# Writing out the ring loops of a graph edge kernel on Trainium2: five hardware loops become straight-line code

## The chip, the cores and the metric

The kernel runs on one core of one Trainium2 chip. Its five engines are TensorE (PE in the profile; its weight loads are PEld), VectorE (DVE), ScalarE (ACT), GpSimd (POOL) and SyncE (SP). Each has its own instruction stream; they meet only in semaphores.
## The reference

There are 12,500 nodes of 64 features and 400,000 edges, sorted by destination.

```
h    = relu(layernorm(x))                       # 12500 x 64
feat = concat(h[dst], h[src] - h[dst])          # 400000 x 128
m    = relu(feat @ W1 + b1) @ W2 + b2           # 400000 x 64
agg  = segment_max(m, dst);  agg = 0 where a node has no edge
out  = x + agg
```

The kernel splits feat @ W1 into a part A of the destination node and a part B of the source node, so that an edge needs relu(A[dst] + B[src]) @ W2. A and B are tables of 12,500 rows in DRAM.

## The kernel before

**Before the ring.** A and B are computed and stored; `a_edges` (400,000 rows) is filled with zeros, and A's row of each node is scattered to that node's first edge. B is also held in SBUF as three bf16 parts (`table`).

**The ring.** Each of the 128 partitions has 3125 edges in order. They are worked on in 260 chunks of 12 edges per partition (1536 edges), and a tail of 5. `RING` = 26 slots of `rows` hold chunks in flight, and `ITERS` = 10 rounds of 26 chunks are the 260 chunks. For chunk c:

- SP: `load_a` waits until `a_fill` is free and loads the chunk of `a_edges` (L333, L334); then it waits for the slot's gathers and loads the indices of the chunk one round later (L342, L343).
- POOL: 11 indirect DMAs gather B[src] for 11 of the chunk's 12 edges (`gather_chunk`, L393). It works up to one round ahead: before it refills a slot, POOL waits for `z_turned` of the chunk that had it, that is until TensorE has transposed it (L436), and for the new indices (L437).
- The 12th edge's B row is picked on TensorE: VectorE splits the index (`split_src`, L920 and L921), ScalarE spreads the keys (L537, L540), TensorE turns them (`turn_keys`, L666), VectorE compares them (`match_keys`, L935), TensorE picks with 37 matmuls of 128x512 into `ps_g` (`pick`, L676), ScalarE masks (`mask`, L549) and VectorE reduces (`choose`, L944).
- DVE: `fill` carries A's row along the edges of a node (12 instructions, L885), `add` forms A + B (L897), `maximum` runs the segmented maximum (12 instructions, L911).
- PE: 6 transposes (L687, they raise `z_turned`), 21 picks, 6 x 2 products with W2 (L696), the key turn (L666) and 16 more picks, the last of which raises `picked`.
- ACT: flags (L530, L531), keys, relu of the transposed sums (L560, waits for `z_turned`), 8 masks (L549), and the store of the chunk's maxima (L567).

In one step, picks are for a chunk 3 ahead and keys for one 5 ahead, so the engines form a loop over neighbouring steps: VectorE's match waits for `picked` of two chunks before; ScalarE's relu for `z_turned`; TensorE's products for the relu.

**What sets the order.** The program is written by hand, engine by engine. Each engine has a hardware loop over the rounds (`Fori`), whose body holds 26 chunks. The round `i` is a register. A semaphore's target that depends on `i`, as `(i * RING + k - RING + 1) * GROUPS`, and an address in DRAM that depends on it, are worked out in registers as the program runs.

Of the kernel before, what the change touches and what calls it, by code (L numbers as in the profile page):

```python
# [18 lines left out]
def edge_conv(nc, x, src, dst, W1, b1, W2, b2, out):  # L19
    N, C = x.shape  # L20
    E = src.shape[0]
    TILES = E // P
    CHUNK = 12
    RING = 26
    ITERS = TILES // (CHUNK * RING)
# [3 lines left out]
    W = CHUNK * C  # L29
# [14 lines left out]
    AE_RING = 2  # L44
# [20 lines left out]
    with ExitStack() as ctx:  # L65
# [18 lines left out]
        state = sb("state", [P, 2, W])  # L84
        zt = sb("zt", [P, GROUPS, 512])
        src_idx = sb("src_idx", [P, RING, CHUNK], I32)
        same = sb("same", [P, TILES + (FILL_AHEAD + 1) * CHUNK])
# [127 lines left out]
        a_loaded = [sem(f"a_loaded{s}") for s in range(AE_RING)]  # L215
# [40 lines left out]
        src_lanes = src.rearrange("(p t) -> p t", p=P)  # L256
        dst_lanes = dst.rearrange("(p t) -> p t", p=P)
        dst_blocks = dst.rearrange("(b k) -> b k", k=BLOCK)
        a_lanes = a_edges.rearrange("(p t) c -> p (t c)", p=P)
# [16 lines left out]
        def _(sp):  # L276
# [55 lines left out]
            def load_a(c, k, tiles=CHUNK):  # L332
                sp.wait_ge(a_free, c + 1)  # L333
                sp.dma_start(a_fill[:, k % AE_RING, 0:tiles * C],  # L334
                             a_lanes[:, bass.ds(c * W, tiles * C)]).then_inc(a_loaded[k % AE_RING], 16)

            with sp.Fori(0, ITERS - 1) as i:
                for k in range(RING):
                    load_a(i * RING + k, k)

                    sp.wait_ge(gathered[k], (i + 1) * 16 * GATHERED)  # L342
                    sp.dma_start(src_idx[:, k, :], src_lanes[:, bass.ds((i * RING + RING + k) * CHUNK, CHUNK)]  # L343
                                 ).then_inc(src_loaded[k // 2], 16)
            for k in range(RING):
                load_a((ITERS - 1) * RING + k, k)
# [22 lines left out]
        def _(pool):  # L369
# [59 lines left out]
                in_=a_table, in_offset=at(dst_all[:, :], 1)).then_inc(ends_gathered, 16)  # L429
            scatter_a(BATCH, NJ)  # L430
            gather_chunk(RING - 1)
            with pool.Fori(1, ITERS) as i:
                for k in range(RING):

                    pool.wait_ge(z_turned, (i * RING + k - RING + 1) * GROUPS)
                    pool.wait_ge(src_loaded[k // 2], (i + 1) * 32)  # L436

                    pool.sem_inc(chunk_open, 1)
                    gather_chunk(k)
# [22 lines left out]
        def _(act):  # L462
# [63 lines left out]

            def flags(c, k, tiles=CHUNK):

                now = same[:, bass.ds(c * CHUNK, CHUNK)]
                nc.scalar.activation(keep[:, k % KEEP, 0, :], now, ACT.Relu)  # L530
                nc.scalar.activation(keep[:, k % KEEP, 1, :], now, ACT.Copy, scale=FLT_MAX).then_inc(keep_ready, 1)  # L531

# [20 lines left out]
            def step(c, k, tiles=CHUNK):  # L553
                if tiles == CHUNK:
                    flags(c + FILL_AHEAD, k + FILL_AHEAD)
                    spread_keys(c + KEYS_AHEAD, k + KEYS_AHEAD)
                for g, n in groups(tiles):
                    act.wait_ge(z_turned, c * GROUPS + g + 1)
                    full = n // 2 * P
                    last = nc.scalar.activation(zt[:, g, 0:full], ps_t[:, g, 0:full], ACT.Relu)  # L560
                    if n % 2:
                        last = nc.scalar.activation(zt[0:C, g, full:full + P], ps_t[0:C, g, full:full + P], ACT.Relu)
                    last.then_inc(relu_done, 1)
                if tiles == CHUNK:
                    mask(c + CHOOSE_AHEAD, k + CHOOSE_AHEAD)
                act.wait_ge(max_step, c * CHUNK + tiles + 1)
                act.dma_start(state_lanes[:, bass.ds(c * W, tiles * C)], state[:, k % 2, 0:tiles * C]  # L567
                              ).then_inc(state_stored[k % 2], 16)

# [26 lines left out]
            for c in range(CHOOSE_AHEAD):  # L597
# [1 line left out]
            act.wait_ge(a_scattered, 16 * NJ)  # L599
            nc.scalar.activation(a_rows[0:NP, :, :], b2_rows[0:NP, :].rearrange("p (o c) -> p o c", o=1)  # L600
                                 .to_broadcast((NP, NJ, C)), ACT.Copy, scale=-1.0).then_inc(maxima_preset, 1)
            with act.Fori(0, ITERS) as i:
                for k in range(RING):
                    step(i * RING + k, k)
            step(CHUNKS, 0, TAIL)
# [5 lines left out]
        def _(pe):  # L611
# [95 lines left out]
            for c in range(-KEYS_AHEAD, 0):  # L707
                turn_keys(c + KEYS_AHEAD, c + KEYS_AHEAD)
                if c >= -PICK_AHEAD:
                    pick(c + PICK_AHEAD, c + PICK_AHEAD, range(PAGES))  # L710
            with pe.Fori(0, ITERS) as i:
                for k in range(RING):
                    step(i * RING + k, k)
            step(CHUNKS, 0, TAIL)
# [8 lines left out]
        def _(dve):  # L723
# [244 lines left out]
            add(0, 0, 0, 0)  # L968
            choose(1, 1)
            fill_all(1)  # L970
            with dve.Fori(0, ITERS) as i:
                for k in range(RING):
                    c = i * RING + k
                    if k + 1 < RING:
                        add(c + 1, k + 1, i, i)
                    else:
                        add(c + 1, 0, i + 1, (i + 1) % ITERS)
                    prepare_picks(c, k, i)
                    fill_ready(c + 2, (k + 2) % RING, i + (k + 2) // RING)

                    dve.wait_ge(state_stored[k % 2], (i * (RING // 2) + k // 2 + 1) * 16)
                    for t in range(CHUNK + LEAD):
                        if t == CHUNK - 2:
                            choose(c + CHOOSE_AHEAD, (k + CHOOSE_AHEAD) % RING)
                        if t < CHUNK:
                            fill(c + 2, (k + 2) % RING, t)
                        if t >= LEAD:
                            maximum(c, k, t - LEAD)
# [45 lines left out]
```

## Time and profile before

| | |
|---|---|
| median of 3 runs | 5047.05 us (5042.66 to 5049.33) |
| the profiled execution | 5046.15 us, of which the span of the trace is 5044.3 us |
| PE, PEld busy | 3240.3 us (64%), 1876.2 us (37%) |
| POOL busy | 3109.6 us (62%) |
| DVE busy | 2493.6 us (49%) |
| ACT busy | 1025.4 us (20%) |
| mean granted TensorE clock | 0.794 of full speed |
| the chain that ended last | "another core or an unknown queue" 41%, "issue" 28%, DVE 10%, ACT 9%, PE 7% |

The first 737 us are the preparation; the ring then runs to about 4890 us, and the end of the kernel (last maxima, output) takes the rest. No engine is busy for more than 64% of the span, and the largest part of the chain is a releaser that the profile can't name. So the shares don't say what limits the ring; the rows of a few chunks must.

### The profile page before, as it was taken

Reading aid. Unit: us, or ns where it says so; the run is one execution under the profiler, and the core shown is the slowest. Engines: PE = TensorE matmul, PEld = TensorE weight load, DVE = VectorE, ACT = ScalarE, POOL = GpSimd, SP = SyncE. Lnnn points to the kernel's source line nnn. Section 1 sums busy time; section 2 is a strip of 40 time slices with the busy share of each in tenths; the row PEclk is TensorE's granted clock in tenths of the full one; section 3 lists DMA queues with packets and bytes.
Section 4 is the critical chain, followed back from the end, with each engine's and each line's share of the span. In section 5 each row is a group of like instructions: output and inputs, shape, how many; then the busy total and the mean of one; then the engine's idle time right before and its main releaser. Section 6 shows DMA issues by size and latency. Waiting matters only on the chain.

```text
span 5044.3 us, 58734 instructions
## 1 busy us (share of the span) xinstructions
PE 3240.3 (64%) x14598; PEld 1876.2 (37%) x14861; DVE 2493.6 (49%) x8363; ACT 1025.4 (20%) x4057; POOL 3109.6 (62%) x3186
## 2 busy tenths in 40 slices
PE   2100137777777777777777777777777777777970
PEld 2100014444444444444444444444444444444540
DVE  4100115555555555555555555555555555556871
ACT  4300212212122121221212222122221212212320
POOL 5777756666666666666666666666666666664017
PEclk8555558888888888888888888888888888888985
DMA  7866312222222222222222222222222222222222
GB/s 274 315 229 227 115 32 73 67 73 70 70 73 67 73 70 70 70 70 73 70 70 69 70 73 69 70 70 69 73 67 73 70 70 72 69 72 71 80 77 56
DMA packets 239614, 452.86 MB, mean 90 GB/s; under 512 B 94781, under 2 KB 95402, under 8 KB 238738
## 3 DMA queue, kind: packets, MB, share of 16 engines
q1 hardware_dynamic: 97663, 225.75, 14.2%
q0 software_dynamic: 103216, 117.29, 11.1%
q10 hardware_dynamic: 38362, 105.62, 5.4%
q8 instruction: 140, 2.29, 0.2%
q14 instruction: 233, 1.91, 0.1%
HBM read 230.84 MB, written 217.71 MB: 89 GB/s over the span
## 4 chain that ended last, share of the span: by engine, by line
another core or an unknown queue 41%; issue 28%; DVE 10%; ACT 9%; PE 7%; POOL 2%; ACTq 2%; DMA 1%; DVEq 1%; POOLq 0%; SPq 0%
ACT dst_all L549 5%; DVE state L911 4%; PE ps_g L676 4%; DVE a_fill L885 3%; PE ps_m L696 2%; POOL a_rows L456 2%; ACT zt L560 2%; ACTq L567 1%; DMA shared<-in_x_dram 1%; DVE rows L897 1%; ACT zt L474 1%; ACT keep L531 1%; PE ps_t L687 0%; ACT shared L501 0%
## 5 line engine op out<-in xcount | busy, mean ns | idle before, releaser
L393 POOL DMA_INDIRECT rows<-b_table,src_idx x2865 | 2785.5, 972 | 1523.6 <-issue 805.7
L676 PE MATMUL ps_g<-shared,dst_all 128*128 128x512 bf16 x9468 | 2318.6, 400 | 174.3 <-issue 170.5
L676 PEld LDWEIGHTS ps_g<-shared,dst_all 128*128 128x128 bf16 x9731 | 1011.1, 105 | 1329.5 <-issue 417.3
L696 PE MATMUL ps_m<-w_diag,zt 128*128 128x128 f32 x3126 | 707.8, 411 | 920.2 <-ACT zt L560 917.8
L696 PEld LDWEIGHTS ps_m<-w_diag,zt 128*128 128x128 f32 x3126 | 638.2, 308 | 1056.3 <-ACT zt L560 1049.8
L911 DVE SCALAR_TENSOR_TENSOR state<-state,keep,ps_m 128x64 f32<-128x64 f32 x3125 | 862.3, 276 | 202.5 <-PE ps_m L696 166.7
L885 DVE SCALAR_TENSOR_TENSOR a_fill<-a_fill,keep 128x64 f32<-128x64 f32 x3144 | 879.6, 280 | 53.1 <-DVE a_fill L885 41.6
L935 DVE TENSOR_TENSOR dst_all<-ps_s,page_keys 128x1664 bf16<-128x1664 f32 x132 | 249.6, 1891 | 816.0 <-remote 795.1
L935 DVE TENSOR_TENSOR dst_all<-ps_x,page_keys 128x1664 bf16<-128x1664 f32 x132 | 249.6, 1891 | 794.7 <-remote 774.7
L560 ACT ACTIVATE zt<-ps_t 128x512 f32<-128x512 f32 (+1 forms) x521 | 226.4, 486 | 1517.9 <-remote 1511.6
L549 ACT ACTIVATE dst_all<-ps_g,dst_all 128x64 f32<-128x64 f32 x2096 | 458.1, 347 | 33.2 <-DVE rows L944 33.2
L530 ACT ACTIVATE keep<-same 128x12 f32 (+1 forms) x263 | 55.9, 213 | 1662.2 <-issue 929.0
L666 PE MATMUL ps_s<-dst_all,ones_h 128*128 128x128 f16 x133 | 40.2, 302 | 442.4 <-ACT dst_all L540 440.9
L897 DVE TENSOR_TENSOR rows<-rows,a_fill 128x512 f32<-128x512 f32 (+1 forms) x522 | 269.1, 557 | 33.2 <-issue 33.2
L944 DVE TENSOR_REDUCE rows<-dst_all 128x64 f32<-128x512 f32 x262 | 267.9, 1023 | 0.0
L687 PE MATMUL ps_t<-ident,rows 128*128 128x128 f32 x1563 | 213.5, 273 | 1.4 <-issue 1.4
L853 DVE TENSOR_TENSOR a_fill<-a_fill,shared 128x512 f32<-128x512 f32 x26 | 18.0, 693 | 383.3 <-issue 372.3
L687 PEld LDWEIGHTS ps_t<-ident,rows 128*128 128x128 f32 x1563 | 186.8, 141 | 53.0 <-issue 3.5
L666 PEld LDWEIGHTS ps_s<-dst_all,ones_h 128*128 128x128 f16 x133 | 19.2, 145 | 442.8 <-issue 440.0
L447 POOL DMA_INDIRECT head<-states,lane_i x1 | 0.9, 942 | 261.2 <-DMA states<-state 261.2
L401 POOL DMA_INDIRECT rows<-in_dst_dram,blk_idx x101 | 102.6, 1016 | 73.5 <-issue 24.4
L419 POOL DMA_INDIRECT a_edges<-a_rows,first_idx x100 | 108.8, 1088 | 31.3 <-issue 31.3
(116 smaller groups left out, 877.0 us busy)
## 6 DMA issues: line engine op xcount, KB each, us to landing
a_edges<-state SPq DMA_DIRECT2D x80, 1250.0 KB
a_fill<-a_edges SPq DMA_DIRECT2D x260, 384.0 KB
states<-state ACTq DMA_DIRECT2D x260, 384.0 KB
rows<-b_table,src_idx POOLq DMA_INDIRECT x2865
src_idx<-in_src_dram SPq DMA_DIRECT2D x234, 6.0 KB
shared<-in_x_dram SPq DMA_DIRECT2D x5, 625.0 KB
b_table<-shared ACTq DMA_DIRECT2D x5, 625.0 KB
a_table<-a_rows SPq DMA_DIRECT2D x1, 3125.0 KB
```

The source lines that it names most:

```text
L393: nc.gpsimd.indirect_dma_start(out=rows[:, slot, t * C:(t + 1) * C], out_offset=None, in_=b_table, in_offset=at(src_idx[:, slot, :], t)).t ...
L419: nc.gpsimd.indirect_dma_start(out=a_edges, out_offset=at(first_idx, j), in_=a_rows[:, j, :], in_offset=None, bounds_check=E - 1, oob_is_e ...
L549: last = nc.scalar.activation(masked[:, o, :], ps_g[:, k % 2, o * C:(o + 1) * C], ACT.Copy, scale=octet_is[:, k % RING, o:o + 1])
L560: last = nc.scalar.activation(zt[:, g, 0:full], ps_t[:, g, 0:full], ACT.Relu)
L676: last = nc.tensor.matmul(ps_g[:, half, :], key_is[:, half, g, :], table[:, g, t, :], start=(g, t) == (0, 0), stop=g == PAGES - 1)
L687: last = nc.tensor.transpose(ps_t[0:m * C, g, a * C:a * C + P], rows[:, k, t * C:(t + m) * C], ident[:, :])
L696: last = nc.tensor.matmul(ps_m[:, g, a * C:(a + m) * C], zt[0:m * C, g, a * C:a * C + P], w2_pair[0:m * C, 0:m * C], start=True, stop=True)
L885: nc.vector.scalar_tensor_tensor(here, before, keep[:, k % KEEP, 0, t:t + 1], here, ALU.mult, ALU.add).then_inc(fill_step, 1)
L897: nc.vector.tensor_tensor(rows[:, k, part], rows[:, k, part], a_fill[:, k % AE_RING, part], ALU.add).then_inc(z_ready, 1)
L911: nc.vector.scalar_tensor_tensor(state[:, half, t * C:(t + 1) * C], before, keep[:, k % KEEP, 1, t:t + 1], ps_m[:, g, r * C:(r + 1) * C], ...
L935: nc.vector.tensor_tensor(key_is[:, half, :, :], ps_k[half].rearrange("p (o e) -> p o e", o=1).to_broadcast((P, PAGES, P)), page_keys[:, : ...
L944: nc.vector.tensor_reduce(rows[:, k, W - C:W], masked[:, :, :].rearrange("p o c -> p c o"), AX_X, ALU.add).then_inc(chosen, 1)
```

## The change

Every `Fori` over the rounds becomes a Python `for`, so `i` is a number when the program is built. The 26-chunk body is written out ten times on ACT, PE and DVE, and nine times on POOL and SP, with each semaphore target and address a constant. What is computed, the waits' targets and the order of engine instructions and DMAs stay as they are. The loop over the clearing of `a_edges` at L315 stays a hardware loop.

```diff
-                             a_lanes[:, bass.ds(c * W, tiles * C)]).then_inc(a_loaded[k % AE_RING], 16)
-
-            with sp.Fori(0, ITERS - 1) as i:
+                             a_lanes[:, c * W:c * W + tiles * C]).then_inc(a_loaded[k % AE_RING], 16)
+
+            for i in range(ITERS - 1):
                 for k in range(RING):
                     load_a(i * RING + k, k)
...
-                    sp.dma_start(src_idx[:, k, :], src_lanes[:, bass.ds((i * RING + RING + k) * CHUNK, CHUNK)]
+                    sp.dma_start(src_idx[:, k, :], src_lanes[:, (i * RING + RING + k) * CHUNK:(i * RING + RING + k + 1) * CHUNK]
...
-            with pool.Fori(1, ITERS) as i:
+            for i in range(1, ITERS):
...
-                now = same[:, bass.ds(c * CHUNK, CHUNK)]
+                now = same[:, c * CHUNK:(c + 1) * CHUNK]
...
-            with act.Fori(0, ITERS) as i:
+            for i in range(ITERS):
...
-            with pe.Fori(0, ITERS) as i:
+            for i in range(ITERS):
...
-            with dve.Fori(0, ITERS) as i:
+            for i in range(ITERS):
```

The instructions of VectorE at the start of the ring: the loop's entry, then chunk 0 up to its match. ISA and REGISTER_ALU are register work, [waits ...] names the semaphores that the row waits for. Before:

```order
L971 ISA
L891 ISA [waits fill_step]
L894 REGISTER_ALU [waits gathered1]
L897 TENSOR_TENSOR rows<-rows,a_fill 128x512 [waits chosen]
L897 TENSOR_TENSOR rows<-rows,a_fill 128x256
L918 REGISTER_ALU
L919 REGISTER_ALU [waits src_loaded2]
L920 TENSOR_SCALAR key_bits<-src_idx 128x1 [waits keys_spread]
L921 TENSOR_SCALAR key_bits<-src_idx 128x1
L933 REGISTER_ALU
L934 REGISTER_ALU [waits keys_turned]
L935 TENSOR_TENSOR dst_all<-ps_s,page_keys 128x1664 [waits picked]
```

And the same place now:

```order
L897 TENSOR_TENSOR rows<-rows,a_fill 128x512 [waits chosen,gathered1,fill_step]
L897 TENSOR_TENSOR rows<-rows,a_fill 128x256
L920 TENSOR_SCALAR key_bits<-src_idx 128x1 [waits keys_spread,src_loaded2]
L921 TENSOR_SCALAR key_bits<-src_idx 128x1
L935 TENSOR_TENSOR dst_all<-ps_s,page_keys 128x1664 [waits picked,keys_turned]
```

The register rows are gone, and the semaphores they waited for stand at the next engine instruction; the order of the others is the same. In one round VectorE's loop body held 415 REGISTER_ALU and 47 ISA, some 18 a chunk.

GpSimd at its loop's entry, the first slots refilled. Before:

```order
L393 DMA rows<-b_table,src_idx 128x64 x11
L432 UNCONDITIONAL_BRANCH
L432 ISA
L436 ISA [waits z_turned]
L393 DMA rows<-b_table,src_idx 128x64 [waits src_loaded0]
L393 DMA rows<-b_table,src_idx 128x64 x10
L435 ISA
```

And now:

```order
L393 DMA rows<-b_table,src_idx 128x64 x11
L393 DMA rows<-b_table,src_idx 128x64 [waits z_turned,src_loaded0]
L393 DMA rows<-b_table,src_idx 128x64 x10
L393 DMA rows<-b_table,src_idx 128x64 [waits z_turned,src_loaded0]
L393 DMA rows<-b_table,src_idx 128x64 x10
```

One register instruction a chunk is gone on GpSimd; its 11 gathers and the two semaphores it waits for are the same.

## Rows read from the trace of the kernel before

**Rows 1.** Windows: span; busy us (count) by engine; PEclk, DMA share, GB/s.

```profile
2035.00:2467.00 432.00, 318.22 (x1430) 185.22 (x1456) 237.47 (x807) 89.38 (x365) 276.25 (x286) 0.84 0.27 70
4760.00:4780.00 20.00, 19.90 (x112) 11.51 (x113) 18.08 (x63) 6.56 (x29) 0.00 (x0) 1.00 0.25 80
```

**Rows 2.** Timeline, two chunks: start us, us, engine, line, operation, [idle before <-releaser].

```profile
2500.12 0.87 ACT L560 ACTIVATE zt<-ps_t 128x512 f32<-128x512 f32 x2 [6.58 <-remote]
...
2500.93 0.94 POOL L393 DMA_INDIRECT rows<-b_table,src_idx  x1 [2.77 <-remote]
...
2502.18 0.98 POOL L393 DMA_INDIRECT rows<-b_table,src_idx  x1 [0.31 <-issue]
...
2508.68 0.82 PE L687 MATMUL ps_t<-ident,rows 128*128 128x128 f32 x6
...
2513.83 0.94 POOL L393 DMA_INDIRECT rows<-b_table,src_idx  x1 [0.30 <-issue]
2516.72 0.87 ACT L560 ACTIVATE zt<-ps_t 128x512 f32<-128x512 f32 x2 [6.63 <-remote]
2516.74 1.89 DVE L935 TENSOR_TENSOR dst_all<-ps_x,page_keys 128x1664 bf16<-128x1664 f32 x1 [7.32 <-remote]
...
2517.54 0.94 POOL L393 DMA_INDIRECT rows<-b_table,src_idx  x1 [2.77 <-remote]
...
2534.16 0.94 POOL L393 DMA_INDIRECT rows<-b_table,src_idx  x1 [2.78 <-remote]
```

**Rows 3.** Timeline, last round of the ring, after GpSimd's last gather.

```profile
4748.35 1.88 DVE L935 TENSOR_TENSOR dst_all<-ps_s,page_keys 128x1664 bf16<-128x1664 f32 x1
...
4755.81 0.82 PE L687 MATMUL ps_t<-ident,rows 128*128 128x128 f32 x6
...
4758.38 1.88 DVE L935 TENSOR_TENSOR dst_all<-ps_x,page_keys 128x1664 bf16<-128x1664 f32 x1
...
4759.04 0.85 ACT L560 ACTIVATE zt<-ps_t 128x512 f32<-128x512 f32 x2
```

**Rows 4.** Waits from 700 to 4800 us: waiter <- releaser: us, times, longest.

```profile
ACT zt L560 <- remote: 1511.6, 233, 7.4
DVE dst_all L935 <- remote: 1490.1, 228, 32.4
...
POOL rows L393 <- remote: 677.9, 234, 3.3
```

**Rows 5.** Sequencer instructions by line: count: duration ns min/median/max.

```profile
L881 DVEq ALU_OP  x2860: 13/40/697, 744.1 to 4885.7; - x191
...
L905 DVEq FUSED_REGOPS  x260: 46/46/64, 745.7 to 4881.8; - x130
...
L334 SPq FUSED_REGOPS  x234: 42/43/703, 697.8 to 4562.9; - x117
...
L435 POOLq FUSED_REGOPS  x216: 37/37/37, 743.0 to 4582.6; - x108
...
L711 PEldq COMPARE_BRANCH  x10: 83/4306/4822, 1157.1 to 4882.8; - x10
```

**Rows 6.** Timeline across a turn of the loops (near 2453 to 2459 us).

```profile
2450.87 0.94 POOL L393 DMA_INDIRECT rows<-b_table,src_idx  x1 [3.17 <-remote]
...
2461.28 1.03 DVE L897 TENSOR_TENSOR rows<-rows,a_fill 128x512 f32<-128x512 f32 x2 [2.96 <-issue]
...
2466.61 1.89 DVE L935 TENSOR_TENSOR dst_all<-ps_s,page_keys 128x1664 bf16<-128x1664 f32 x1 [4.18 <-remote]
2466.67 0.87 ACT L560 ACTIVATE zt<-ps_t 128x512 f32<-128x512 f32 x2 [1.52 <-remote]
...
2467.56 0.94 POOL L393 DMA_INDIRECT rows<-b_table,src_idx  x1 [3.18 <-remote]
...
2484.30 0.94 POOL L393 DMA_INDIRECT rows<-b_table,src_idx  x1 [3.01 <-remote]
```

More of the change, by code:

```diff
@@ L566, in step @@
                 act.wait_ge(max_step, c * CHUNK + tiles + 1)
-                act.dma_start(state_lanes[:, bass.ds(c * W, tiles * C)], state[:, k % 2, 0:tiles * C]
+                act.dma_start(state_lanes[:, c * W:c * W + tiles * C], state[:, k % 2, 0:tiles * C]
                               ).then_inc(state_stored[k % 2], 16)
```

## Prediction

> **What bounds the kernel now.** I read the slices of the page first, then windows, two chunks of the timeline, the waits, and last the sequencers' own instructions.
>
> The windows show two regimes. While GpSimd gathers, a round of 26 chunks takes 432 us, 16.6 us a chunk, and no engine is full: PE is busy for 318 of the 432 us, POOL for 276, DVE for 237. After the last gather PE is busy for 19.90 of 20 us at full clock [rows 1], and a chunk takes 4758.38 - 4748.35 = 10.03 us [rows 3]. That stage is bound by TensorE's own work. Some 234 chunks are of the first kind and 26 of the second.
>
> In the first regime the timeline shows a fixed beat. The relus start at 2500.12 and 2516.72, 16.60 us apart; GpSimd's first gathers of a chunk at 2500.93, 2517.54 and 2534.16, 16.61 and 16.62 us apart [rows 2]. Each beat is made of GpSimd's parts: 11 gathers at 1.25 us from start to start (the first at 2500.93, the eleventh at 2513.83, ending at 2514.77), then 2.77 us of waiting. 2514.77 - 2500.93 = 13.84, and with 2.77 it is 16.61.
>
> What is it that GpSimd waits for? By the code `z_turned`, raised by TensorE's transposes. Those run from 2508.68 to 2509.50, yet ScalarE's relu, which waits for the same semaphore, starts at 2516.72, 7.2 us after they end, and VectorE's match, which waits for `picked`, at 2516.74 [rows 2]. GpSimd follows 0.8 us later. In the stage without gathers the relu starts 4759.04 - 4756.63 = 2.4 us after the transposes [rows 3]. So three engines on three semaphore waits come free together, about 2 us after GpSimd's last gather of the chunk ends, and only while it gathers. The profile has no name for what holds TensorE's signals back ("remote"), in 233 of ScalarE's waits (1511.6 us), 228 of VectorE's and 234 of GpSimd's [rows 4]. I take it as a beat that GpSimd's 11 gathers set: burst, release, next burst. Whatever the other engines do within 16.6 us ends in a wait.
>
> **The change part by part.** The sum is made against the profiled execution, 5046.15 us (span 5044.3); the median of the runs shown is 5047.05, 0.9 us above it.
>
> *Register work on VectorE.* 415 + 47 instructions a round are 18 a chunk, at 40 ns (L881) to 46 ns (L905) [rows 5]: 18 x 40 = 0.72 us a chunk of sequencer time, 187 us over 260 chunks. They run while the datapath is busy with the instruction before, or within the wait of 7.32 us before the match [rows 2]. Value: 0. If that cover were gone it would be all of 0.72 us in the 234 chunks, 168 us. In the last stage PE is full, so it is 0 there too.
>
> *Register work on the others.* SyncE loses some 5 to 6 a chunk at about 43 ns (L334) and GpSimd 1 at 37 ns (L435) [rows 5]; the one on GpSimd is issued ahead, while gathers are running. TensorE loses 3 and ScalarE 6 a chunk (83 and 159 a round in the order of instructions), which I price like the row of L435. All lie ahead of a wait. Value: 0; together at most 15 x 0.04 = 0.6 us a chunk, 140 us, if all of it stood in the beat, which no row suggests.
>
> *The wait itself.* GpSimd needs 0.81 us from the release seen on ScalarE (2516.72) to its first gather (2517.54). It waits for the same two semaphores after the change, before the same DMA, so that stays, as do the 11 gathers: they had constant addresses already. Bounds: 0 below, and above the 37 ns of its register instruction, 9 us over 234 chunks.
>
> *The turns.* A branch on TensorE takes 4.31 us in the median, ten times [rows 5]. At the turn shown VectorE comes to its add 2.96 us late, and then waits 4.18 us for the match instead of 7.32, ScalarE 1.52 us for the relu instead of 6.63: the waits absorb it [rows 6]. GpSimd's beats across that turn are 2467.56 - 2450.87 = 16.69 and 2484.30 - 2467.56 = 16.74 us against 16.61: 0.08 + 0.13 = 0.21 us a turn, 1.9 us for nine. If the waits didn't cover them, 4.31 x 9 = 39 us would come back. I take 1.9, since the beats across the turn show it directly.
>
> The Trainium skill has a rule that speaks for more ("Runtime: NRT & Kernel Launch", Instruction fetch mechanics): fetch runs ahead in straight order, a taken branch out of the loaded pages stalls for a fetch, and therefore kernels prefer to be unrolled. The 4.31 us of the branch agrees with the stall. By that rule alone the sum would be 39 us; by the rows of the beat it is 2.
>
> *Entry of the loops.* Around 697 to 707 us some of SyncE's register instructions take up to 0.70 us each (the maximum of L334) [rows 5]. Five or six of them before the first chunk would be 3 to 4 us if TensorE waited behind them; 0 if not. I take 1.
>
> *Code.* The straight-line code is longer as a program, but every instruction of a loop was executed ten times anyhow; the number executed falls by the register work. No added wait, no added DMA, no order changed. Value 0.
>
> Sum: 1.9 + 1 = 2.9 us off: 5043.3 for a profiled execution, 5044 us for a median.
>
> **The rivals.**
>
> *A. The turns are exposed.* Then 39 us come off, 5008 us. For it: branches of 4.31 us. Against it: the shrunken waits of rows 6. Chance 0.10.
>
> *B. The beat gets shorter.* If TensorE's signals are held back because something that all the sequencers share is loaded (they all fetch and signal), removing the register work relieves it. For it: up to 0.70 us for a register instruction that has a median of 43 ns, on an engine that touches no data [rows 5]; the hold has no other name. Against it: the beat follows GpSimd's gathers, which don't change. A beat shorter by the 0.04 to 0.72 us of the bounds above gives 9 to 168 us, 4879 to 5038; were the hold gone altogether, GpSimd would be at 13.84 + 0.3 of issue gap, 2.47 us shorter in 234 chunks: 578 us, 4468. Chance 0.20 in all, of which 0.03 is the whole hold, and about half stands in the first 55 us.
>
> *C. The beat gets longer: slower.* The gathers' hold is met sooner: VectorE and TensorE, rid of 0.72 us a chunk, raise `picked` and `z_turned` earlier in the burst, and if each held signal costs a further step of the 0.70 us that the longest register instructions took [rows 5], the beat is 17.3 us in 234 chunks: +164 us, 5211. One chunk in three of that is 55 us, 5102. It decides once GpSimd's first gathers stand more than 16.62 us apart. Against it: the beat was the same whether VectorE's match came free with the relu or not. Chance 0.12 for slower by over 0.2%.
>
> *D. The change doesn't do what it says.* The order of instructions shows that it does; 0.
>
> **How the numbers follow.** My forecast, the beat unmoved, has 0.58. Two runs of this kernel differ by up to 7 us, so under 0.2% (10 us) can't be told from no change. The forecast's own range is 5034 to 5054, nearly all of it within 0.2%. A (0.10) and B (0.20) are faster; the forecast lends a little to each side. Faster 0.31, same 0.55, slower 0.14. The range goes down to A and into B's first third, 4990, and up to 5062, a part of C: 0.58 + 0.10 + 0.10 + 0.03, about 0.8.
>
> **What would show it.** Right: GpSimd's first gathers still 16.6 us apart, ScalarE's relu still some 7 us behind the transposes' end, the last stage still at 10.03 us a chunk, DVE's and ACT's waits longer by what the register work was, and no beat of 16.7 at the old turns. A would show as rounds shorter by 4 us at the turns alone. B or C would show as another beat in every chunk, with GpSimd's wait of 2.77 us shorter or longer and its gathers still 1.25 us apart. The forecast is wrong if that wait changes by more than 0.05 us a chunk.

## The result, and the profile after

The changed kernel is slower: 5086.52 us in the median of six runs (5072.64 to 5103.61), against 5044.82 us (5039.43 to 5049.33) for the kernel before on the same chip, ratio 1.0089 with a 95% interval of [1.0066, 1.0112]. The forecast was 5044 with a range of 4990 to 5062, and slower had a chance of 0.14. The profiled execution took 5083.08 us, its span is 5081.3 us, 37.0 us above the span before; the granted clock is nearly the same (0.796 against 0.794). The change did what it says: 50,057 instructions instead of 58,734, and no register instruction left on PE, ACT or DVE.

The page's groups of the kernel after. Columns: busy us, mean ns of one | idle us before it, and what ended most of that.

```profile
L676 PE MATMUL ps_g<-shared,dst_all 128*128 128x512 bf16 x9468 | 2498.8, 410 | 643.0 <-issue 620.0
L911 DVE SCALAR_TENSOR_TENSOR state<-state,keep,ps_m 128x64 f32<-128x64 f32 x3125 | 860.0, 275 | 1370.6 <-remote 1023.0
L560 ACT ACTIVATE zt<-ps_t 128x512 f32<-128x512 f32 (+1 forms) x521 | 232.7, 483 | 748.3 <-remote 697.4
L393 POOL DMA_INDIRECT rows<-b_table,src_idx x2865 | 2777.2, 969 | 1565.5 <-issue 835.0
```

The same groups on the page of before, which were not shown ahead:

```profile
L676 PE MATMUL ps_g<-shared,dst_all 128*128 128x512 bf16 x9468 | 2318.6, 400 | 174.3 <-issue 170.5
L911 DVE SCALAR_TENSOR_TENSOR state<-state,keep,ps_m 128x64 f32<-128x64 f32 x3125 | 862.3, 276 | 202.5 <-PE ps_m L696 166.7
L560 ACT ACTIVATE zt<-ps_t 128x512 f32<-128x512 f32 (+1 forms) x521 | 226.4, 486 | 1517.9 <-remote 1511.6
L393 POOL DMA_INDIRECT rows<-b_table,src_idx x2865 | 2785.5, 972 | 1523.6 <-issue 805.7
```

Read the last row of each first. GpSimd's gathers take as long as before (8 us less in all), and its idle time ahead of them grew by 41.9 us: 33.6 of the 37.0 us stand there. By the gathers' starts and ends, the ring's first one starts 2.7 us later, from there to the end of the ring's last one it takes 3914.4 us instead of 3886.4, and what follows is 6.2 us longer. Then see how the waits of the others changed places. VectorE used to wait ahead of the key match [rows 4] and hardly ahead of its maxima (202.5 us); now it waits 1370.6 us ahead of the maxima, and TensorE, which waits for nothing the profile can name ("issue"), has 643.0 us of gaps between picks instead of 174.3. These two rows don't say where the time went: the kernel before, run again (e5 below), has 864.2 us ahead of the maxima too, and e8, which is faster than before, has 521.3 us of TensorE's gaps.

GpSimd's waits from 700 to 4800 us, kernel after, answering to [rows 4]. Columns: waiter <- releaser: us in total, times, longest.

```profile
POOL rows L393 <- issue: 746.9, 2379, 8.1
POOL rows L393 <- remote: 457.0, 167, 4.8
POOL rows L393 <- PE ps_t L687: 273.5, 36, 38.1
```

Before, 234 waits of 2.90 us in the mean ended "remote", one at each chunk's end. Now only 167 do, and 36 end at TensorE's transposes; without the first one (38.1 us, ahead of the ring; 35.2 us before) those are 35 waits of 6.7 us. Between them are places where GpSimd does not wait at all: from the starts of its gathers, 35 times 22 gathers follow each other without a pause, which never happened in the profile before.

The price of such a pair can be added up from the 233 pauses between bursts. Before they are 2.90 us in the mean, 675 us together. After, 36 are under 1 us (0.32 us in the mean), the pause that follows one of these is 6.7 us in the mean, and the others are 2.9 us as before: 714 us together. So a pair first saves 2.6 us and then costs 3.8 us, 1.3 us net, and 36 of them explain the 39 us by which the pauses grew.

One such pair, the third of the 35, in the timeline after (start us, us, engine, line, operation, [idle before <-releaser]):

```profile
904.89 1.89 DVE L935 TENSOR_TENSOR dst_all<-ps_s,page_keys 128x1664 bf16<-128x1664 f32 x1 [1.94 <-remote]
...
909.83 1.11 ACT L560 ACTIVATE zt<-ps_t 128x512 f32<-128x512 f32 x2 [6.20 <-remote]
...
911.34 0.94 POOL L393 DMA_INDIRECT rows<-b_table,src_idx  x1 [2.99 <-remote]
...
915.43 0.82 PE L687 MATMUL ps_t<-ident,rows 128*128 128x128 f32 x6
...
917.99 1.88 DVE L935 TENSOR_TENSOR dst_all<-ps_x,page_keys 128x1664 bf16<-128x1664 f32 x1
...
919.26 0.60 ACT L560 ACTIVATE zt<-ps_t 128x512 f32<-128x512 f32 x1 [0.51 <-remote]
...
925.33 0.94 POOL L393 DMA_INDIRECT rows<-b_table,src_idx  x1 [0.30 <-issue]
...
929.91 0.58 PE L676 MATMUL ps_g<-shared,dst_all 128*128 128x512 bf16 x1 [3.29 <-issue]
...
931.31 0.61 PE L676 MATMUL ps_g<-shared,dst_all 128*128 128x512 bf16 x1 [0.82 <-issue]
...
932.74 0.59 PE L676 MATMUL ps_g<-shared,dst_all 128*128 128x512 bf16 x1 [0.82 <-issue]
...
937.82 0.94 POOL L393 DMA_INDIRECT rows<-b_table,src_idx  x1 [0.30 <-issue]
...
942.70 0.28 DVE L911 SCALAR_TENSOR_TENSOR state<-state,keep,ps_m 128x64 f32<-128x64 f32 x1 [21.75 <-remote]
...
946.98 1.06 POOL L393 DMA_INDIRECT rows<-b_table,src_idx  x1 [8.21 <-PE ps_t L687]
```

At 904.89 VectorE gets its picks in the middle of GpSimd's burst, so it meets the match about 5 us ahead of ScalarE's relu; in [rows 2] both came free together after the burst. (Alone this breaks nothing, as e5 shows below.) Its part is then already done when the relu comes (909.83), and the next chunk runs fast: the relu is again at 919.26, 9.4 us later, as in the stage that TensorE bounds. So `z_turned` is there before GpSimd's burst, begun at 911.34, has ended. GpSimd goes on without a pause (0.30 us before the gather at 925.33), to 938.76. In the second half of these 22 gathers TensorE crawls: single matmuls 1.40 and 1.43 us apart, with 0.82 us of gap though they wait for no semaphore. Its next transposes, which come after these picks, start only at 944.68, and so GpSimd itself waits 8.21 us for them. VectorE gets the products of TensorE only at 942.70, after 21.75 us, though the last of the twelve started at 924.92: that signal was late, whatever TensorE's pace. The windows around it (span, then busy us (count) of PE, PEld, DVE, ACT, POOL; granted clock, DMA share, GB/s), the first to be held against [rows 1]:

```profile
2035.00:2467.00 432.00, 318.69 (x1427) 167.32 (x1452) 237.27 (x814) 89.21 (x364) 271.35 (x282) 0.84 0.26 70
4790.00:4810.00 20.00, 19.89 (x112) 11.46 (x113) 18.00 (x62) 6.64 (x28) 0.00 (x0) 1.00 0.24 78
894.00:920.00 26.00, 21.20 (x108) 12.45 (x111) 17.36 (x60) 7.57 (x29) 17.32 (x18) 0.93 0.25 68
920.00:947.00 27.00, 13.30 (x43) 5.57 (x43) 5.07 (x23) 2.02 (x9) 14.22 (x17) 0.62 0.16 35
918.00:924.00 6.00, 4.43 (x24) 2.72 (x23) 2.77 (x7) 3.23 (x12) 4.55 (x5) 1.00 0.57 158
930.00:936.00 6.00, 2.87 (x5) 0.45 (x5) 0.00 (x0) 0.00 (x0) 4.48 (x6) 0.50 0.15 30
```

The 27 us of the crawl hold 43 matmuls against 108 in the 26 us ahead, and the granted clock is 0.62 against 0.93. The clock did not start the crawl: it is still at its full level (1.00, 2.4 GHz) from 918 to 924, where the first single matmul stands after a gap (922.81), and at the lower one (0.50, 1.2 GHz) from 930, after TensorE had worked for only 0.62 of 6 us. A late fetch of code doesn't set the pace either: the pages count 271 packets in the two instruction queues after and 373 before, and the one such packet that the trace has in the crawl, at 932.98, lies between matmuls that are 1.40 us apart ahead of it (929.91 and 931.31) and behind it (938.37 and 939.77).

The long window of 432 us shows nothing: a round that lost and one that didn't look alike in it, POOL's 282 gathers against 286 aside. The last stage is unchanged at 4816.34 - 4806.31 = 10.03 us a chunk, its relu 4806.97 - 4804.56 = 2.4 us behind the transposes, as in [rows 3]:

```profile
4803.74 0.82 PE L687 MATMUL ps_t<-ident,rows 128*128 128x128 f32 x6
4806.31 1.88 DVE L935 TENSOR_TENSOR dst_all<-ps_s,page_keys 128x1664 bf16<-128x1664 f32 x1
4806.97 0.85 ACT L560 ACTIVATE zt<-ps_t 128x512 f32<-128x512 f32 x2
...
4816.34 1.88 DVE L935 TENSOR_TENSOR dst_all<-ps_x,page_keys 128x1664 bf16<-128x1664 f32 x1
```

### The profile page after: what moved, and what is told of

It is laid out like the page before. It is cut to its first block, busy times and chain, and to the rows that moved or that the text cites. A ratio compares the mean times of both kernels' runs of the same rounds, so it can differ in the third digit from the quotient of the medians.

```text
span 5081.3 us, 50057 instructions
## 1 busy us (share of the span) xinstructions
PE 3251.7 (64%) x14598; PEld 1711.5 (34%) x14861; DVE 2484.5 (49%) x8363; ACT 1026.7 (20%) x4057; POOL 3098.0 (61%) x3186
## 3 DMA queue, kind: packets, MB, share of 16 engines
q14 instruction: 153, 1.25, 0.1%
## 4 chain that ended last, share of the span: by engine, by line
another core or an unknown queue 30%; PE 27%; issue 21%; DVE 13%; ACT 5%; POOL 2%; DMA 1%; ACTq 0%; DVEq 0%; POOLq 0%; SPq 0%
PE ps_g L676 20%; PE ps_m L696 6%; DVE state L911 5%; DVE a_fill L885 5%; POOL a_rows L456 2%; PE ps_t L687 2%; ACT dst_all L549 1%; DVE rows L897 1%; ACT zt L560 1%; DMA shared<-in_x_dram 1%; ACT zt L474 1%; ACT dst_all L540 1%; ACT shared L501 0%; ACTq L567 0%
## 5 line engine op out<-in xcount | busy, mean ns | idle before, releaser
L676 PE MATMUL ps_g<-shared,dst_all 128*128 128x512 bf16 x9468 | 2498.8, 410 | 643.0 <-issue 620.0
L676 PEld LDWEIGHTS ps_g<-shared,dst_all 128*128 128x128 bf16 x9731 | 987.7, 103 | 1979.3 <-issue 1132.4
L911 DVE SCALAR_TENSOR_TENSOR state<-state,keep,ps_m 128x64 f32<-128x64 f32 x3125 | 860.0, 275 | 1370.6 <-remote 1023.0
L696 PE MATMUL ps_m<-w_diag,zt 128*128 128x128 f32 x3126 | 525.5, 326 | 388.3 <-ACT zt L560 251.4
L696 PEld LDWEIGHTS ps_m<-w_diag,zt 128*128 128x128 f32 x3126 | 479.9, 233 | 493.4 <-ACT zt L560 308.5
L530 ACT ACTIVATE keep<-same 128x12 f32<-128x12 f32 x263 | 55.9, 212 | 2406.3 <-DVE state L911 1737.6
L687 PE MATMUL ps_t<-ident,rows 128*128 128x128 f32 x1563 | 245.9, 290 | 55.7 <-issue 54.9
L687 PEld LDWEIGHTS ps_t<-ident,rows 128*128 128x128 f32 x1563 | 203.4, 150 | 136.2 <-issue 93.0
```

The costliest lines, as they stand in the source:

```text
L676: last = nc.tensor.matmul(ps_g[:, half, :], key_is[:, half, g, :], table[:, g, t, :], start=(g, t) == (0, 0), stop=g == PAGES - 1)
L687: last = nc.tensor.transpose(ps_t[0:m * C, g, a * C:a * C + P], rows[:, k, t * C:(t + m) * C], ident[:, :])
L696: last = nc.tensor.matmul(ps_m[:, g, a * C:(a + m) * C], zt[0:m * C, g, a * C:a * C + P], w2_pair[0:m * C, 0:m * C], start=True, stop=True)
L911: nc.vector.scalar_tensor_tensor(state[:, half, t * C:(t + 1) * C], before, keep[:, k % KEEP, 1, t:t + 1], ps_m[:, g, r * C:(r + 1) * C], ...
```

## The experiments

Ratios are to the kernel before on the same chip, where it took 5011 us for e1 to e8 and 5053 to 5057 us for e9 to e18. The last columns are counted in the profiled execution, over the 234 chunks of the ring in which GpSimd gathers: the mean time from GpSimd's first gather of a chunk to that of the next (its beat), the times from one key match to the next that are over 22 us, the pairs of bursts that GpSimd issued without a pause (one or two more or less by what is called a pause, in e12 from 18 to 30), and the relus of ScalarE that start before the burst under way has ended.

| run | what | ratio, 95% | beat | over 22 us | pairs | relus in a burst |
|---|---|---|---|---|---|---|
| before | | | 16.62 | 0 | 0 | 2 |
| after | all five written out | 1.0089 [1.0066, 1.0112] | 16.74 | 51 | 35 | 116 |
| e1 | SyncE alone | 1.0009 [0.9998, 1.0019] | 16.50 | 5 | 4 | 14 |
| e2 | TensorE alone | 1.0042 [1.0022, 1.0062] | 16.58 | 14 | 12 | 47 |
| e3 | VectorE alone | 1.0102 [1.0071, 1.0134] | 16.61 | 45 | 33 | 117 |
| e4 | ScalarE alone | 1.0006 [0.9997, 1.0016] | 16.48 | 3 | 2 | 10 |
| e5 | before again | 1.0004 [0.9995, 1.0014] | 16.49 | 3 | 3 | 12 |
| e6 | after, 11 registers a chunk in VectorE's fill waits | 1.0047 [1.0033, 1.0061] | 16.54 | 47 | 31 | 116 |
| e7 | before, 8 gathers a chunk | 0.8049 [0.8037, 0.8062] | 12.29 | 0 | 0 | 12 |
| e8 | after, GpSimd waits for its own gathers | 0.9790 [0.9776, 0.9803] | 16.03 | 11 | 0 | 107 |
| e9 | before, with that wait | 1.0000 [0.9990, 1.0009] | 16.68 | 0 | 0 | 2 |
| e10 | after again | 1.0071 [1.0054, 1.0088] | 16.83 | 47 | 36 | 120 |
| e11 | all but VectorE | 0.9982 [0.9973, 0.9992] | 16.63 | 3 | 2 | 9 |
| e12 | as e8, for ten of eleven | 1.0054 [1.0037, 1.0070] | 16.70 | 48 | 28 | 118 |
| e13 | after, VectorE's waits from registers | 0.9978 [0.9969, 0.9988] | 16.61 | 1 | 1 | 4 |
| e14 | after, one such wait a chunk | 1.0054 [1.0036, 1.0073] | 16.83 | 41 | 32 | 104 |
| e15 | e8 again | 0.9888 [0.9870, 0.9906] | 16.43 | 53 | 0 | 121 |
| e16 | after, 8 gathers a chunk | 0.8082 [0.8067, 0.8097] | 12.48 | 14 | 14 | 46 |
| e17 | after, 19 idle registers a chunk on VectorE | 0.9984 [0.9975, 0.9994] | 16.61 | 2 | 2 | 6 |
| e18 | after, pause within the burst | 1.0009 [0.9997, 1.0021] | 16.49 | 41 | 0 | 182 |

**One engine at a time.** e1 to e4 are the kernel before with one loop written out, as the diff does it. The times expected are for a chip on which before takes 5045 us, so the ratios are to be compared. In e3:

```diff
-            with dve.Fori(0, ITERS) as i:
+            for i in range(ITERS):
```

> Only SyncE's loop is written out. Theory 1 (TensorE's signals leave late while GpSimd gathers, in steps of 0.7 us that SyncE's and TensorE's own instructions take up; with fewer of them `picked` gets out early, VectorE starts a step early and the fixed beat breaks): SyncE loses 5 to 6 instructions a chunk, so the beat breaks, chunks of about 9.2 us and of over 23 us appear, and the time is 5065 to 5100. Theory 2 (VectorE's or ScalarE's steps became quicker, and that alone breaks the beat): the beat stays at 16.6 us, 5045 +- 8.

> Only TensorE's loop is written out. Theory 1: TensorE loses 3 register instructions of some 120 a chunk, so at most a part of the effect: 5045 to 5075. Theory 2: 5045 +- 8, beat 16.6 us in every chunk.

> Only VectorE's loop is written out. Theory 1: VectorE's register instructions don't use what TensorE's signals wait for: 5045 +- 8, beat 16.6 us. Theory 2: VectorE loses 18 instructions a chunk, 0.72 us; the beat breaks, 5065 to 5100.

> Only ScalarE's loop is written out. Theory 1: 5045 +- 8, beat 16.6 us. Theory 2: a smaller part of the effect than VectorE's, 5045 to 5070.

VectorE alone costs as much as all five, TensorE alone some of it, SyncE and ScalarE nothing that can be measured. The first theory, that the other sequencers' own instructions are what the hold works on, falls with e1. VectorE's row for e3 is that of the kernel after:

```profile
L911 DVE SCALAR_TENSOR_TENSOR state<-state,keep,ps_m 128x64 f32<-128x64 f32 x3125 | 861.5, 276 | 1347.1 <-remote 982.8
```

**Is the rhythm of before luck?** e5 is the kernel before, unchanged.

> The kernel before, unchanged, beside itself. Both theories: ratio 1.000 within 0.001. The theory of the broken beat (the 16.6 us rhythm holds as long as VectorE meets the matches in step with GpSimd's burst, and every second burst that follows without a pause costs) expects the start of the key match to come every 16.5 to 16.7 us in nearly all of the 234 chunks, as in the first profile, and no pair of bursts without a pause. The rival, that the rhythm of the first profile was luck of one execution and that any execution may fall out of it, expects a few double bursts here too.

Its ratio is 1.0004, but it has three pairs, where the first profile had none. So the loops don't forbid them, they make them rare, and e1's and e4's few are those of before. Two rows of its page and one chunk of its timeline:

```profile
L676 PE MATMUL ps_g<-shared,dst_all 128*128 128x512 bf16 x9731 | 2426.9, 406 | 128.9 <-issue 127.5
L911 DVE SCALAR_TENSOR_TENSOR state<-state,keep,ps_m 128x64 f32<-128x64 f32 x3125 | 861.0, 276 | 864.2 <-PE ps_m L696 638.6
```

```profile
2511.11 1.89 DVE L935 TENSOR_TENSOR dst_all<-ps_s,page_keys 128x1664 bf16<-128x1664 f32 x1 [3.62 <-remote]
2512.23 0.95 POOL L393 DMA_INDIRECT rows<-b_table,src_idx  x1 [0.30 <-issue]
2515.29 0.87 ACT L560 ACTIVATE zt<-ps_t 128x512 f32<-128x512 f32 x2 [7.13 <-remote]
2516.11 0.95 POOL L393 DMA_INDIRECT rows<-b_table,src_idx  x1 [2.93 <-remote]
```

Here too the match (2511.11) comes within the burst, 4 us ahead of the relu, and the rhythm holds. In e5 205 of 235 matches do, in the first profile 55, in the changed kernel 157. What sets the changed kernel apart is the relu, that is `z_turned`: 2 relus before, 12 in e5 and 116 after start while a burst is still going on (last column). Of the runs with bursts of 11, those whose VectorE has some 18 register instructions a chunk (e1, e4, e11, e13, e17) have 4 to 14 of them, those with none, one or eleven 104 to 121, e2, with all of them, 47, and e18, with a pause in each burst, 182.

**All but VectorE.** e11 is the changed kernel with VectorE's `Fori` kept.

> The changed kernel, but VectorE keeps its loop. If VectorE's loop is what keeps the rhythm (e3 lost 1.0% by it alone, e2 0.4% by TensorE's, SyncE's and ScalarE's nothing), this should cost what TensorE's alone did: ratio 1.002 to 1.006, 8 to 20 double bursts. If the engines' parts add up independently of VectorE: 1.006 to 1.010.

0.9982 and two pairs: the other four, TensorE's too, cost nothing while VectorE keeps its loop; they even save 0.2%. That is better than either theory expected. TensorE's share in e2 and VectorE's in e3 don't add up.

**What of VectorE's loop is it?** e6 adds a register that holds zero to the target of the fill waits, e14 to that of the match's wait for `picked` alone, e13 to nearly all (here e6):

```diff
+            zero_reg = dve.alloc_register("zero_reg")
+            dve.reg_mov(zero_reg, 0)
...
-                    dve.wait_ge(fill_step, c * CHUNK + t)
+                    dve.wait_ge(fill_step, c * CHUNK + t + zero[0])
```

> All loops written out as in the changed kernel, but VectorE's eleven fill waits a chunk get their value from a register again (a register that holds zero is added to the constant), 2860 register instructions of some 40 ns, no branch. Theory V1, that VectorE's register instructions hold its step back (some 0.45 us a chunk) and so keep the match behind GpSimd's burst: the beat locks again, ratio to before 1.000 to 1.003, under five double bursts. Rival V2, that it is something else of the loop (where instructions lie, the branch's pause that resets the phase every 26 chunks): the time stays that of the changed kernel, ratio 1.006 to 1.011, thirty or more double bursts.

> All loops written out as in the changed kernel, but each wait of VectorE's ring gets its value from a register again (the round's number is a register that holds zero plus a constant), just the register work of before, and no branch. Theory V1b, that the register work as a whole (not only the fill waits') keeps the match in step: ratio to before under 1.002 and under ten double bursts, beside e6's 1.0047 and 29. Rival V2, that VectorE's register work is a part at most and TensorE's loop and the lay-out of the code do the rest: 1.003 to 1.008, 15 or more double bursts.

> As e10 was meant to be: all loops written out, and nearly every wait of VectorE's ring takes its value from a register (5046 register instructions in the ring instead of the 4620 of before, no branch). In e10 the register held a known zero and its instructions folded away (the program had none), so e10 was the changed kernel once more. Theory V1b, that VectorE's register work as a whole keeps the match in step with GpSimd's burst: ratio under 1.002, under ten double bursts. Rival V2, that something else of the loop does: 1.004 to 1.010, 25 or more double bursts.

> All loops written out, and only the key match's wait for the picks takes its value from a register (one register instruction a chunk). Theory V1c, that the one place matters where VectorE waits for TensorE's picks (45 ns there put the match behind a signal that is held): 1.000 to 1.003, under ten double bursts. If no single place matters: as the changed kernel, 1.006 to 1.010, 30 or more.

e6 came out between its two expectations in time, with the pairs of the changed kernel; but the pause after a skipped one is 6.1 us there, against 6.7 us after and 7.1 us in e10. e10 carries no register instruction and so is a second measurement of the changed kernel, 1.0071; what it was meant to test, e13 tested: 0.9978 and one pair, though no loop and no branch is left (VectorE's ring has 4572 register instructions by the trace, not the 5046 expected). V1b holds, the one wait of V1c does not. But is it that a wait takes its value from a register, or the instruction in the stream? e17 keeps all waits constant:

```diff
+                    for _ in range(5):
+                        idle_alu()
                     for t in range(CHUNK + LEAD):
+                        idle_alu()
```

where `idle_alu` adds 3 to a register or masks it, which nothing in the ring reads.

> The changed kernel, and 19 register instructions a chunk in VectorE's step (4940 in all, against e13's 5046) that feed no wait: five ahead of the fills and one ahead of each fill or maximum; all waits keep their constants. If the instructions as such keep the rhythm (VectorE's sequencer is later by some 0.04 us at each): as e13, ratio 0.996 to 1.002, under ten double bursts, idle time ahead of the maxima under 900 us. If it is that a wait takes its value from a register: as the changed kernel, 1.005 to 1.010, 25 or more double bursts, some 1370 us ahead of the maxima.

It is the instructions as such: 0.9984, two pairs. The rows of e13 and e17, to be held against 1370.6 us and 643.0 us after. In e13:

```profile
L676 PE MATMUL ps_g<-shared,dst_all 128*128 128x512 bf16 x9468 | 2314.1, 401 | 147.3 <-issue 143.2
L913 DVE SCALAR_TENSOR_TENSOR state<-state,keep,ps_m 128x64 f32<-128x64 f32 x3125 | 861.7, 276 | 756.5 <-PE ps_m L696 644.9
```

and in e17:

```profile
L393 POOL DMA_INDIRECT rows<-b_table,src_idx x2865 | 2770.7, 967 | 1535.3 <-issue 830.2
L676 PE MATMUL ps_g<-shared,dst_all 128*128 128x512 bf16 x9468 | 2319.3, 401 | 161.8 <-issue 157.3
L911 DVE SCALAR_TENSOR_TENSOR state<-state,keep,ps_m 128x64 f32<-128x64 f32 x3125 | 860.0, 275 | 833.5 <-PE ps_m L696 699.3
```

TensorE's gaps are back at 147 to 162 us, and VectorE's waits end at TensorE's products instead of "remote". Some 4900 register instructions that do nothing are worth about 1% here.

**Do the gathers set the beat?** e7 and e16 gather 8 of 11 tiles a chunk in the ring and leave three ungathered, with the targets of `gathered` to match.

```diff
-                    gather_chunk(k)
+                    gather_chunk(k, 8)
```

> The kernel before with 8 instead of 11 gathers a chunk in the ring (three tiles of a chunk are left ungathered; everything else runs). If GpSimd's burst sets the beat (burst 13.84 us and 2.77 us of hand-over), the beat falls by 3 x 1.25 = 3.8 us to about 12.8 us and the time by 234 x 3.8 = 880 us, to some 4130 us. If something else of the chunk (the round trip of the picks through VectorE, ScalarE and TensorE) needs 16.6 us, the beat stays and the time falls by under 100 us. In between (beat 14 to 15 us, 4400 to 4650 us) means that signals are late for a reason besides the burst's length.

> The changed kernel with 8 instead of 11 gathers a chunk in the ring (three tiles of a chunk stay ungathered), to be compared with e7, the same with the loops (4032.6 us, ratio 0.805, beat 12.3 us, no double bursts). If written-out code loses by double bursts whatever their length (16 in a row, PE's signals held for 19 us): 4050 to 4110 us, with bursts of 16 in a tenth of the chunks. If the rhythm holds with short bursts: 4010 to 4035 us, no bursts of 16, and what the writing-out saves on register instructions is seen alone.

The beat of e7 is 12.29 us and as even as before, a little lower than expected: three gathers less take off 4.3 us, 3 x 1.25 in issue and the rest in a shorter wait, 2.18 us instead of 2.77:

```profile
2520.76 0.94 POOL L393 DMA_INDIRECT rows<-b_table,src_idx  x1 [2.18 <-remote]
...
2533.05 0.94 POOL L393 DMA_INDIRECT rows<-b_table,src_idx  x1 [2.18 <-remote]
```

So the burst sets the beat, and the picks' round trip has room. Written out (e16) the short bursts pair up too: 14 bursts of 16 gathers and 14 times over 22 us, where e7 has none, and a beat of 12.48 us. Its ratio is 0.8082 against 0.8049, intervals apart; but the two ran on different chips, and e8 and e15 below show one kernel's ratio move by 0.01 from chip to chip, so the ratios alone don't show the loss.

**Keeping GpSimd from going on.** e8 is the changed kernel and, ahead of each burst in the ring, a wait for the last chunk's gathers to land:

```diff
                     pool.wait_ge(src_loaded[k // 2], (i + 1) * 32)
+                    pool.wait_ge(gathered[(k - 1) % RING], (i + 1 if k else i) * 16 * GATHERED)
```

> The changed kernel, and GpSimd waits before a chunk's gathers until the last chunk's have landed, so that it never issues 22 without a pause. If the double bursts are what costs (TensorE's, SyncE's and VectorE's signals held for 25 us in them), the periods over 22 us go and the mean period falls from 16.81 to 16.6 us or less: 4960 to 5020 us on this chip, where before takes 5011. If the double bursts only follow from an early chunk before them and the mean is set elsewhere, the wait only moves the time: ratio 1.006 to 1.015 to before. It can cost too: if the landing comes 2 us after the last issue and was not covered, up to 234 x 0.5 us = 117 us more.

> The kernel of e8 again. Its gain is of the kernel and not of one chip or execution: ratio 0.976 to 0.984, mean beat 15.8 to 16.0 us. e12, whose pause is shorter by 1.2 us, lost 0.5% on another chip; if e8's gain was chance, this comes out at 0.99 or more.

> The kernel before with its loops, and the same added wait of GpSimd for its last chunk's gathers as in e8. Theory W1, that the wait takes the place of the rhythm (GpSimd's pause, some 2 us after its last issue, lets the held signals through at once, whoever loops): the time falls as in e8, ratio 0.977 to 0.984, beat near 13.84 + 2.0 = 15.9 us. Rival W2, that e8 gained because the written-out engines could use the pause and the loops cannot: 0.995 to 1.003. The difference between this run and e8 is what the writing-out itself is worth when the rhythm no longer depends on it: W1 with e8's figure says under 0.3%.

> As e8, but GpSimd waits before a chunk's gathers only for the first ten of the last chunk's eleven; the eleventh counts on a semaphore of its own. The pause shrinks from 3.3 us between issues (e8's median) to some 2.1 us. If the signals get through in a pause that short, the beat falls by up to 1.2 us to 14.7 us and the time by up to 280 us from e8's 4901, to 4640 to 4800. If the pause must be longer, signals are held again and double bursts (here one with a short pause inside) cost as in the changed kernel: 4900 to 5060.

e8 is faster than both kernels, 4900.90 us, 2.1% under before. On another chip the same kernel (e15) gains 1.1%, 4997.84 us: the sign holds, the expected ratio did not. GpSimd's waits in e8:

```profile
POOL rows L393 <- issue: 793.5, 2379, 2.5
POOL rows L393 <- remote: 329.0, 138, 3.0
...
POOL rows L393 <- DMA rows<-b_table,src_idx: 127.2, 51, 4.3
POOL rows L393 <- PE ps_t L688: 63.7, 12, 38.2
```

Summed from its gathers' starts and ends, GpSimd's pauses over 1.2 us between gathers come to 560 us in e8 and 655 us in e5 on the same chip; none in e8 is over 4.3 us, while the kernel after has 28 over 5 us, 203 us together. e9 shows that the wait does nothing for the kernel with loops (1.0000): there each of the 234 waits ends "remote", as before, and none at a landing. What gains is written-out code, in which `z_turned` gets through within a burst, together with a pause that GpSimd can't skip. W1 falls, W2 holds. With one gather less to wait for (e12) the gain is gone, the pairs are back, and the time is 5083.6 us. The expected times went by e8's chip; there e12's ratio would be some 5038 us (1.0054 x 5011), within the second expectation. e10, the changed kernel once more, took 5095.93 us on the chip on which e15 took 4997.84, 1.9% less.

e15 also corrects the story: it has 53 times over 22 us, as many as the kernel after, and no pair. Long periods come with bursts of 11 too; what the added wait removes are GpSimd's own long waits. Nor does it stop TensorE's crawl. In e8, within a burst of 11 and at full clock (1.00 from 2912 to 2926 us):

```profile
2915.96 0.94 POOL L393 DMA_INDIRECT rows<-b_table,src_idx  x1 [0.30 <-issue]
2916.84 0.38 PE L677 MATMUL ps_g<-shared,dst_all 128*128 128x512 bf16 x1 [1.02 <-issue]
2918.24 0.38 PE L677 MATMUL ps_g<-shared,dst_all 128*128 128x512 bf16 x1 [1.02 <-issue]
...
2919.22 0.94 POOL L393 DMA_INDIRECT rows<-b_table,src_idx  x1 [2.32 <-DMA rows<-b_table,src_idx]
```

Neighbouring matmuls 1.3 to 1.5 us apart come 26 times in the ring before, 268 times after (125 of them past the eleventh gather of a pair), 220 times in e8, and 5 and 13 times in e13 and e17. They come with the early relus and not only with the pairs.

**A pause inside the burst.** e18 waits after six gathers until they have landed; the last five count on a semaphore of their own.

> The changed kernel, and GpSimd waits after six of a chunk's eleven gathers until those six have landed; the last five count on a semaphore of their own. A pause inside each burst lets TensorE's, SyncE's and VectorE's signals through after six gathers, so no hold is longer than some eight gathers' time even where two bursts follow each other. If the holds are what is paid for: no periods over 22 us, mean beat 13.84 + 2.0 to 13.84 + 3.0 us, time 4860 to 5090 us, the lower half if GpSimd need not wait again at the chunk's end. If the pause only comes on top of the 2.77 us that GpSimd waits anyway: beat 18.6 us, 5500 us.

The time fell inside the expected range and is that of before. But the edit also put the pause into the 26 chunks that are gathered ahead of the ring: the ring's first gather starts at 783.2 us, against 740.8 us in e17 on the same chip. In the ring itself e18 takes 3857.7 us against 3884.1 us, 26 us less (one execution each). So in the ring the pause seems to gain 0.7% on a kernel with the rhythm kept, though at 124 of the 233 ends of a burst GpSimd doesn't wait at all. 41 times are over 22 us, against the expected none: what the theory said of the held signals is not borne out.

## Why the prediction was wrong

- **The step that failed** is "Register work on VectorE ... Value: 0", with its ground, "Whatever the other engines do within 16.6 us ends in a wait". The cover was there as far as VectorE's own instructions go: its maxima and fills take 275 and 279 ns as before (276 and 280). What failed is that GpSimd's wait of 2.77 us, and with it the order of the signals, was taken as given. Without VectorE's register instructions `z_turned` gets through within the burst in 116 chunks instead of 2; 36 times GpSimd skips its pause, saves 2.6 us, and pays 3.8 us at the next. In place of 0 the step was worth +0.9%: e3 has it alone (1.0102), e13 and e17 take it back (0.9978, 0.9984). That it is this register work is shown; how it keeps `z_turned` back is not. The early match is not the way, since e5, e13 and e17 have it in 205 to 220 chunks and keep the rhythm.
- **The bounds** of that step were 0 and a gain of 168 us. No loss was in them, and the range's upper end came from C alone.
- **"A beat that GpSimd's 11 gathers set"** was right: 16.6 us with 11, 12.29 us with 8, and 10.03 us without any. It was read from one execution in which it never failed; e5 has three failures in 234 chunks.
- **Rival C** had the mechanism in part: signals are "met sooner" and the kernel is slower. Its price, 0.70 us in every chunk or in one of three, is not what happened: 36 pauses are skipped, 36 are of 6.7 us, the others are as before, and the mean pause is 3.06 us instead of 2.90, 0.16 us a chunk. The text's own mark for a wrong forecast, 0.05 us a chunk, was passed.
- **The turns, 1.9 us.** With the rhythm kept, writing out all loops saves 0.22% (e13) or 0.16% (e17), 8 to 11 us, where the sum had 2.9 us with the entry. The Trainium skill's rule that kernels prefer to be unrolled since a taken branch out of the loaded pages stalls ("Runtime: NRT & Kernel Launch", Instruction fetch mechanics) would have been 39 us; the branches of TensorE are gone in e2 and that run is slower. A's 39 us are refuted. Of B only its smallest end can be true: e13's beat is 16.61 us beside 16.68 in e9 on the same chip, each from one execution, and the time saved is 0.2%.
- **The rest** stands: the last stage at 10.03 us, and the gathers 1.25 us apart.

What stays open: why some 19 instructions of 40 ns on VectorE's sequencer decide whether `z_turned` gets through in the middle of a burst; why eleven of them make the long pauses shorter (e6) and not fewer; why TensorE's loop written out alone costs 0.4% (e2) and with those of SyncE, ScalarE and GpSimd nothing (e11); and what holds TensorE and its signals while GpSimd gathers.

## What to carry to other kernels

Where engines wait for each other in a ring and the profile shows one regular beat with a wait that it can't name, that beat is a state of the system and not a property of one engine: making an engine that always waits faster can break it, and the loss can land on another engine, as it did here on GpSimd. Bound such an edit on both sides of zero, and look in more than one execution for rare long waits, because windows of hundreds of microseconds hide them. Where an engine skips a wait and pays more at the next one, try an explicit wait (here on its own DMAs) instead of relying on the others to be late. In written-out code that was worth 1.1 to 2.1% here, with the loops nothing (e9), and with one gather less to wait for 0.5% was lost (e12), so such a wait has to be measured in its place. And add up the pauses of the engine that sets the beat: the waits of the others moved by hundreds of microseconds without moving the time.

## What the runs showed that was not expected

- While GpSimd issues indirect DMAs, TensorE's matmuls without any semaphore can stand 1.40 us apart: 0.59 us of work and 0.82 us of gap at the lower clock (931.31 us after), 0.38 and 1.02 us at the full one (2916.84 us in e8, in a burst of 11). Between 920 and 947 us the granted clock is 0.62.
- Register instructions that nothing reads make a kernel faster: 4940 of them on VectorE take the changed kernel from 1.0071 (e10) to 0.9984 (e17), on two chips by ratios to before.
- The kernel before takes 5011 us on two of the chips and 5045 to 5057 us on others; ratios near one moved less than that, but e8's gain halved from one chip to another.
